# First aggregation in two halves, five layer norms in later slots, four weight turns one slot later, in a four-layer graph network on one core

## What is computed

```
L0:  y = adj @ x + x;  y = y @ weight + bias;  y = y / max(norm(y), EPS)
L1:  five times:  m = adj @ h;  av = [m, m]
        z = sigmoid(av @ w3.T + b3 + u3);  r = sigmoid(av @ w4.T + b4 + u3)
        hv = tanh(av @ w5.T + b5 + (r*h) @ u5.T + ub5);  h = (1-z)*h + z*hv
L2:  out = (D (adj + I) D) @ x @ W.T + b
L3:  A = softmax(where(adj > 0, e[index of the edge], NEG));  out = diag(A) x W0 + offdiag(A) x W1 + bias
x = layernorm(x + L0(x));  x = layernorm(x + L1(x));  x = layernorm(x + L2(x));  x = layernorm(x + L3(x))
```

## Time and profile before

| | us |
|---|---|
| median of 3 runs | 761.27 (760.66 to 761.44) |
| the profiled execution | 761.36 |
| its span, first to last instruction | 759.3 |
| PE busy in it | 748.2 (99%) |
| DVE busy | 638.2 (84%) |
| ACT busy | 503.1 (66%) |
| POOL busy | 160.4 (21%) |

### The profile page before, as it was taken

How to read it: one execution, slowest core, us unless ns; L and a number is a source line. 1 busy time by engine, 2 the same in 40 slices (tenths; PEclk the granted TensorE clock), 3 DMA queues, 4 the chain that set the end, 5 groups by cost and what they waited for, 6 DMA issues and landing times.

```text
span 759.3 us, 11936 instructions
## 1 busy us (share of the span) xinstructions
PE 748.2 (99%) x3768; PEld 627.3 (83%) x3768; DVE 638.2 (84%) x1473; ACT 503.1 (66%) x1047; POOL 160.4 (21%) x307
## 2 busy tenths in 40 slices
PE   8999999999999999999999999999999999999996
PEld 7888788888888888888888888888888888788886
DVE  5899998888888998877777788777999999787775
ACT  4899777666666676666666666666587857864433
POOL 1878420000000000000000000000122258654333
PEclk9999999999999999999999999999999999999999
DMA  6500000000031001000000000000000000101112
GB/s 207 226 1 2 1 1 1 1 1 1 0 119 15 0 2 56 1 0 1 1 0 0 0 0 0 0 1 2 0 1 2 1 0 2 28 2 43 56 42 84
DMA packets 11605, 17.12 MB, mean 23 GB/s; under 512 B 4512, under 2 KB 6048, under 8 KB 10912
## 3 DMA queue, kind: packets, MB, share of 16 engines
q1 hardware_dynamic: 11552, 16.47, 6.5%
HBM read 9.12 MB, written 5.25 MB: 19 GB/s over the span
## 4 chain that ended last, share of the span: by engine, by line
PE 80%; DVE 9%; ACT 6%; POOL 2%; issue 2%; DMA 1%; SPq 0%; POOLq 0%; ACTq 0%; DVEq 0%
PE agg_ps L1073 12%; PE agg_ps L1075 12%; PE agg_ps L1074 12%; PE gate_ps L982 6%; PE gate_ps L984 6%; PE gate_ps L983 6%; PE cand_ps L982 4%; PE cand_ps L984 4%; PE cand_ps L983 4%; PE turn_ps L1112 4%; PE gate_ps L989 3%; PE cand_ps L989 3%; DVE stats L873 1%; ACT res L453 1%; PE turn_ps L1116 1%
## 5 line engine op out<-in xcount | busy, mean ns | idle before, releaser
L1073 PE MATMUL agg_ps<-adj_hi,nat_hi 128*128 128x512 f32 x384 | 152.1, 396 | 0.0
L1075 PE MATMUL agg_ps<-adj_hi,nat_lo 128*128 128x512 f32 x384 | 150.2, 391 | 0.0
L1074 PE MATMUL agg_ps<-adj_lo,nat_hi 128*128 128x512 f32 x384 | 149.6, 390 | 0.0
L653 POOL TENSOR_SCALAR shift<-mean_var 128x4 f32<-128x4 f32 x62 | 24.4, 394 | 408.6 <-DVE mean_var L877 406.4
L827 DVE TENSOR_TENSOR agg_lo<-agg_ps,agg_hi 128x512 fp32r<-128x512 f32 x80 | 55.2, 690 | 57.6 <-ACT agg_hi L488 57.6
L524 ACT ACTIVATE reset_hi<-gate_r 128x512 fp32r<-128x512 f32 x80 | 50.6, 633 | 78.0 <-DVE gate_r L844 78.0
L505 ACT ACTIVATE gate_r<-gate_ps,bias 128x512 f32<-128x512 f32 x80 | 55.2, 690 | 48.6 <-PE gate_ps L984 48.6
L1075 PEld LDWEIGHTS agg_ps<-adj_hi,nat_lo 128*128 128x128 f32 x384 | 72.1, 188 | 16.2
L1074 PEld LDWEIGHTS agg_ps<-adj_lo,nat_hi 128*128 128x128 f32 x384 | 72.2, 188 | 15.6
L1073 PEld LDWEIGHTS agg_ps<-adj_hi,nat_hi 128*128 128x128 f32 x384 | 72.1, 188 | 15.1
L488 ACT ACTIVATE agg_hi<-agg_ps 128x512 fp32r<-128x512 f32 x80 | 48.6, 608 | 44.1 <-PE agg_ps L1075 43.8
(11 more groups left out here) (205 smaller groups left out, 1757.0 us busy)
## 6 DMA issues: line engine op xcount, KB each, us to landing
res<-in_x SPq DMA_DIRECT2D x16, 256.0 KB, 5.8
out<-res SPq DMA_DIRECT2D x16, 256.0 KB, 2.0
rows<-in_adj SPq DMA_DIRECT2D x4, 256.0 KB, 4.5
adj_hi<-eye_hi SPq DMA_DIRECT2D x1, 1024.0 KB, 10.1
adj_lo<-eye_lo SPq DMA_DIRECT2D x1, 1024.0 KB, 11.8
later<-in_adj SPq DMA_DIRECT2D x1, 1024.0 KB, 6.6
mix_rows<-mix SPq DMA_DIRECT2D x1, 1024.0 KB, 8.1
later<-mix_rows SPq DMA_DIRECT2D x1, 1024.0 KB, 4.8
```

What stands on the lines that cost most here:

```text
L1073: pe.matmul(ps, nat_hi[:, b, k, :], m_hi[:, k, :], start=(k == 0), stop=False)
L1074: pe.matmul(ps, nat_hi[:, b, k, :], m_lo[:, k, :], start=False, stop=False)
L1075: last = pe.matmul(ps, nat_lo[:, b, k, :], m_hi[:, k, :], start=False, stop=(k == T - 1))
```

## The change

Three edits. (1) At the start, `x[0]` is loaded after two row blocks instead of after four; ACT splits it before block 1 instead of before block 3; the masks of blocks 2 and 3 go to the end of DVE's start; and unit 0's aggregation is done in two halves of 256 columns, 24 matmuls instead of 12, the first four of them before block 3 is transposed. (2) For the L0 units 11 to 15 the stages stats, norm, split, cross and back come 1, 2, 3, 4 and 5 slots later. (3) `MIX_AT` is 106 instead of 105, and DVE reads a mix turn before a back turn where both fall into one slot.

```
+LAST_PROMPT = 10
...
     if what == "add" and B - 2 <= u < B:
         return 1
+    if stage(u) == L0 and what in ("stats", "norm", "split", "cross", "back"):
+        return LAGS[what][0] + max(0, u - LAST_PROMPT)
     return LAGS[what][0 if stage(u) == L0 else 1 if is_step(u) else stage(u) - L2 + 2]
...
-MIX_AT = EXP_AT + T
+MIX_AT = EXP_AT + T + 1
...
             for t in range(T):
+                if t == T // 2:
+                    load_x(0)
                 sp.dma_start(rows[:, t, :], adj.rearrange("(p t) m -> t p m", t=T)[t]).then_inc(adj_in[t], 16)
-            load_x(0)
...
             for t in range(T):
-                if t == T - 1:
+                if t == 1:
                     act.wait_ge(x_in[0], 16)
                     act.activation(nat_hi[:, 0, :, :], res[:, 0, :, :], ACT.Copy).then_inc(x_hi_made, 1)
...
-            for t in range(T):
+            def mask_rows(t):
                 dve.wait_ge(adj_in[t], 16)
                 dve.tensor_scalar(mask[:, t * N:(t + 1) * N], rows[:, t, :], 0.0, None, ALU.is_gt).then_inc(mask_made, 1)
-                if t == T - 1:
+
+            for t in range(T):
+                if t < 2:
+                    mask_rows(t)
+                if t == 1:
                     x_lo(0)
                 dve.wait_ge(eye_hi_made, t + 1)
...
-            for b in range(1, 3):
-                x_lo(b)
+            x_lo(1)
+            x_lo(2)
+            mask_rows(2)
+            mask_rows(3)
...
+            def first_sums(half, part):
+
+                cols = slice(half * (N // 2), (half + 1) * (N // 2))
+                x, m = (nat_lo if part == 1 else nat_hi), (eye_lo if part == 2 else eye_hi)
+                for k in range(T):
+                    last = pe.matmul(agg_ps[0][:, cols], x[:, 0, k, :], m[:, k, cols], start=part == 0 and k == 0,
+                                     stop=part == 2 and k == T - 1)
+                return last
+
+            for t in range(3):
+                turn_chunk(t)
+            pe.wait_ge(eye_lo_made, 1)
+            pe.wait_ge(eye_hi_made, 2)
+            pe.wait_ge(x_hi_made, 1)
+            first_sums(0, 0)
+            turn_chunk(3)
+            pe.wait_ge(x_lo_made, 1)
+            first_sums(0, 1)
+            pe.wait_ge(eye_lo_made, 2)
+            first_sums(0, 2)
+            pe.wait_ge(eye_hi_made, T)
+            first_sums(1, 0)
+            first_sums(1, 1)
+            pe.wait_ge(eye_lo_made, T)
+            first_sums(1, 2).then_inc(agg_done, 1)
```

More of the change, by code:

```diff
@@ L726, in turn_of @@
                     return turn_ps[TURN_NO[key] % 2]
+                k = s - 1 - MIX_AT
+                if 0 <= k < T:
+                    dve.wait_ge(mix_hi_made, k + 1)
+                    dve.tensor_tensor(adj_lo[:, k, :], turn_ps[TURN_NO["mix", k] % 2][:, :],
+                                      adj_hi[:, k, :].bitcast(F32), ALU.subtract).then_inc(turn_read, 1)
                 for n in norms_at(s, "back"):
@@ L734, in slot @@
                                           ALU.mult).then_inc(turn_read, 1)
[L735 to L739, removed]
                 if s == BEFORE_AT + 1:
@@ L968, in turn_rows, with turn_chunk @@
                 return last
-            for t in range(T):
+            def turn_chunk(t):
                 pe.wait_ge(adj_in[t], 16)
@@ L1037, in slot @@
             def slot(s, ahead):
-                if s < UNITS:
+                if 0 < s < UNITS:
                     if s < B:
-                        if s:
-                            pe.wait_ge(x_lo_made, s + 1)
+                        pe.wait_ge(x_lo_made, s + 1)
                     elif 2 * B <= s < AFTER:
@@ L1056, in slot @@
                     b, ps = s % B, agg_ps[s % 2][:, :]
[L1057 to L1075, removed]
+                    for k in range(T):
+                        if s == AFTER + B:
+                            pe.wait_ge(turn_read, reads(TURN_NO["mix", k]))
+                        pe.matmul(ps, nat_hi[:, b, k, :], m_hi[:, k, :], start=(k == 0), stop=False)
+                        pe.matmul(ps, nat_hi[:, b, k, :], m_lo[:, k, :], start=False, stop=False)
+                        last = pe.matmul(ps, nat_lo[:, b, k, :], m_hi[:, k, :], start=False, stop=(k == T - 1))
                     last.then_inc(agg_done, 1)
```

## The result

The changed kernel takes **763.04 us** (median of 10 runs, 761.45 to 763.78) against 761.08 (10 runs, 760.66 to 761.66): a ratio of 1.0022 over all these runs (the means are 762.79 and 761.07), 95% interval 1.0014 to 1.0031. It is slower by 2.0 us in the medians and 1.7 in the means, and the median is 0.04 us outside the range that I gave. I had forecast no change.

A forecast was written before the change was run, and what follows sets the result against it. The prediction took PE as the bound, busy 748.2 of 759.3 us. Its terms, -0.25 - 1.3 + 3.1 - 1.75 = -0.2 us, took the profiled 761.36 to 761.2; it forecast 761.1 us, range 758.4 to 763.0.

The forecast's parts named there:

- Three turns in slot 27: Slot 27: the chosen turn waits for DVE's `nat_lo`, PE stands 3.0 us; 3.1 us lost, bounds 0 to 4.0.
- The start: Start, up to unit 1: PE's idle time is filled, 0.25 us saved; bounds 0.4 saved to 2.3 lost.
- The pitch of the half matmuls: Unit 0's aggregation at the start: half matmuls of 256 columns take 0.12 us each.
- `x[0]` has pushed the last row block 0.6 us back: Loads at the start: same rhythm in the new order, row block 2 at 8.06 and row block 3 at 8.7 us.
- The rival of halves at the pitch of full matmuls: Start: halves take 0.235 us each, unit 1 starts at 15.2, in all +2.5, 763.8 us; chance 0.04.
- Slots 18 to 20: Spreading the stages removes PE's late starts there: 1.3 us saved, bounds 0.4 to 1.8.
- all four late starts: PE's late starts in slots 18 to 20, 1.66 us in sum, put down to a backlog on ACT and DVE.
- The mix turns: Mix turns one slot later: the 1.68 us wait for the last exponential goes; 1.75 us saved, bounds 1.0 to 1.9.
- two turns, not three ... no wait by the rule: Slot 109: last mix turn and first back turn of L2 share it, readers early in slot 110; no wait claimed.
- a wait follows in slots 106 to 112: Sign that the mechanism is wrong: another PE wait within these slots; no size given.
- the wait would not cost what it should: Rival, slot 27: wait costs below 1.6 of the 3.1 us; time 758.0, up to 759.6; chance 0.20.
- DVE could not take the spread work: Rival, from slot 20 on: PE waits for `reset_lo`, `nat_lo` later in slot 27; 763.1 to 764.1 us; chance 0.13.

The follow-up runs named there:

- Runs 5: The changed kernel with 12 useless matmuls of 512 columns issued in slot 27 ahead of the chosen turn, where PE stood still: 762.10 us.
- run 6: The changed kernel with the update gate's product of slot 27 (3 matmuls) issued ahead of the turns instead of behind them: 761.12 us.
- run 7: The kernel of run 1 with a wait for DVE's `nat_lo` added on PE in slot 22, which has one turn: 763.60 us.
- run 2: The kernel before with the edit at the start alone: 760.47 us, ratio 0.9995.
- run 1: The changed kernel with unit 15's cross and back one slot later, so that no slot holds three turns: 758.66 us, ratio 0.9968.
- Run 10: The kernel of run 8 with ACT's four squares of unit 15 issued ahead of `reset_hi` in slot 17: 757.09 us, ratio 0.9954.
- run 8: The kernel of run 1 with exponentials and mix turns both one slot earlier: 758.27 us.
- run 4: The kernel before with the mix turns one slot later alone: 759.91 us, ratio 0.9988.
- run 9: The kernel of run 8 with only units 13 to 15 spread (`LAST_PROMPT = 12`) and no turn moved: 758.24 us.
- run 3: The kernel before with the later stages of L0 units 11 to 15 alone: 763.65 us, ratio 1.0039.

## Why the prediction was wrong

- **Three turns in slot 27: the step that failed.** The place, the wait and its length were right: 3.0 us against 3.1, `nat_lo` as the releaser, nothing locked up. What failed is "I stay at the row's value, since every term of it is a row of this very slot": the rows told how long PE would stand, but none of them told at what pitch PE goes on after standing; I had put that cost at nothing without a reason, and the bound at 4.0 for a late DVE alone. Measured, the place costs 3.0 us where the clock holds and 4.6 where it falls (the three runs up to 762.15 have a mean of 761.7, the other seven 763.25, which is 1.6 more). Before, no wait of PE past the start is over 1.7 us, so the trace held no example. Runs 5, 6 and 7 show the mechanism. The Trainium skill, "TensorE: Matmul & The Clock Gate", section "What's actually happening", says that the throttled state is the default and that activity lifts it, that the clock has two levels, and that the moment of the rise varies from run to run, since the monitor runs free of the kernel. The traces agree on the levels (0.43 and 0.23 us between 512-column matmuls). Of the fall they show that it, too, comes in some executions of one program and not in others (the two groups of times).
- **The start.** Forecast 0.25 saved, 0.4 at most; measured 0.55 in the times of run 2 and 0.9 in the profiled pair. The pitch of the half matmuls (0.12) and the stretch from block 2 to unit 1 (4.38 against 4.37) were right. Mis-sized was "`x[0]` has pushed the last row block 0.6 us back": the row blocks' landings are not a fixed rhythm. With this edit PE began block 2 at 7.45 in the changed kernel, at 7.83 in run 2 and at 8.11 in run 1, where I had 8.08. The rival of halves at the pitch of full matmuls is out.
- **Slots 18 to 20.** Forecast 1.3, measured 0.7 by the times and 0.5 in the trace. I took all four late starts as the backlog's doing and asked only what DVE would be rid of; I asked what is late next only for the mix turns, and there of ACT alone. It was POOL's `length`, which the backlog had hidden. Run 10 brings the rest in: it saves 0.9 us more than run 8, each against the runs of the kernel before beside it (760.80 - 757.09 = 3.7 against 761.06 - 758.27 = 2.8).
- **The mix turns.** Forecast 1.75, measured 1.1 (run 4). The old wait went as forecast. My reading of the last one, "two turns, not three ... no wait by the rule", looked at the wrong pair: the back turn of slot 109 is number k, the last mix turn k-1, and the third mix turn k-2, whose readers run in slot 109 itself, behind ACT's norms. That a wait follows in slots 106 to 112 was one of my own signs of a wrong mechanism, and it came.
- **The rivals.** That the wait would not cost what it should is out: it cost all of it, and more. That DVE could not take the spread work is out too: `nat_lo` starts 3.1 us behind its state turn (153.25 in the trace), 3.0 before, there is no wait for `reset_lo` in slots 20 to 28, and run 9 shows no difference for two norms fewer.

Together: -0.55 - 0.7 - 1.1 + 3.0 + 7/10 of 1.6 = +1.8 us, the measured difference being 1.7 in the means (a share of the runs calls for means) and 2.0 in the medians. My sum had -3.3 and +3.1. Of the miss, 0.95 lies in the savings, two of which uncovered a wait just behind the removed one, and 1.1 in the clock. Without the clock's part the sum is +0.7 us, an estimate, and inside my range; so neither error alone would have led out of it.

## What to carry to other kernels

Where PE is the bound, price a stand of some 3 us as the stand plus what the half clock may take behind it (here 1.6 us for a stand of 3), and look for its cost in the pitch of the matmuls, not in the list of waits. With two banks in turn, count turns by k-2 and not by slot, and move one turn rather than fill a slot with three: that alone turned 2 us lost into 2.4 us gained. When a backlog is removed, look at every engine that it was hiding, since the next wait sits right behind.

## What the runs showed that I had not expected

- The clock does not fall in each execution of the same program: three of ten runs of the changed kernel and two of seven of run 7 kept 0.998 or over with a stand of 3 us, so that one kernel has two times, some 1.6 us apart. Run 3 is less clear: only two of its six runs lie at the time of a fallen clock, so the share of executions is not well known from so few. Behind the stand of 1.7 us of run 6 none of 11 runs shows it. Waits between 1.7 and 2.8 us were not tried.
- Single runs at 0.996 or 0.997 and 1.8 to 2.6 us over the median of their kernel also turned up without a stand of 3 us: one of 11 each in runs 2 and 4 (762.62, 762.48), and one of the 65 of the kernel before (762.88). Their traces were not taken, so what let the clock fall there is open. Seven of ten and five of seven are another matter.
- The fall can come after PE is back at work: in run 3's trace three products passed at nearly full pitch before the first gap of 0.43.
- Twelve matmuls for nothing, in the place of a stand, made the kernel 0.9 us faster.
